# Attention row tiles: the reciprocal of a tile's sums, its spreading and its transposes, one unit later

## What is computed

```python
q, k, v = proj(Wq, bq), proj(Wk, bk), proj(Wv, bv)
scores = jnp.einsum('bhqd,bhkd->bhqk', q, k) * SCALE
scores = scores * (adj_matrix + bond_matrix)[:, None, :, :]
attn = jax.nn.softmax(scores, axis=-1)
ctx = jnp.einsum('bhqk,bhkd->bhqd', attn, v)
out = jnp.einsum('bse,fe->bsf', ctx, Wo) + bo
```

## Time and profile before

| | us |
|---|---|
| median of 3 runs | 2968.77 |
| lowest and highest | 2966.88 and 2968.87 |
| the profiled execution | 2966.04 |
| its span, first to last instruction | 2962.9 |
| TensorE busy | 2841.6 (96%) |
| VectorE busy | 1856.5 (63%) |
| ScalarE busy | 1486.9 (50%) |
| GpSimd busy | 721.2 (24%) |

### The profile page before, as it was taken

One profiled execution on the slowest core, in us unless ns is written; L12 is line 12 of the kernel. 1 busy time (PEld: TensorE's weight loads), 2 busy tenths in 40 slices (PEclk: granted clock), 3 DMA queues, 4 the chain that ended last, 5 costly groups with the idle time before them and its releaser, 6 DMA issues.

```text
span 2962.9 us, 62026 instructions
## 1 busy us (share of the span) xinstructions
PE 2841.6 (96%) x21888; PEld 2255.5 (76%) x21888; DVE 1856.5 (63%) x4010; ACT 1486.9 (50%) x2761; POOL 721.2 (24%) x1305
## 2 busy tenths in 40 slices
PE   8999999999999999999999999999999999999999
PEld 6777787787877878778687786877868778687786
DVE  3787427874288742887428864388643886438862
ACT  2883318833288232873228732387323873238622
POOL 0342003420034201342013420134101441014410
PEclk9999999999999999999999999999999999999999
DMA  5552215522165131651316513155122551226500
GB/s 176 186 165 93 90 61 191 162 91 107 50 201 168 69 129 39 201 178 49 136 45 197 181 50 122 63 189 180 63 101 77 189 181 65 82 81 197 169 8 15
DMA packets 198987, 355.12 MB, mean 120 GB/s; under 512 B 22033, under 2 KB 126865, under 8 KB 198673
## 3 DMA queue, kind: packets, MB, share of 16 engines
q1 hardware_dynamic: 197136, 346.81, 35.1%
q0 software_dynamic: 1536, 4.20, 0.4%
HBM read 212.25 MB, written 84.15 MB: 100 GB/s over the span
## 4 chain that ended last, share of the span: by engine, by line
PE 70%; DVE 15%; issue 8%; ACT 3%; SPq 2%; DMA 1%; DVEq 1%; POOL 0%; ACTq 0%; POOLq 0%
PE ps L1265 37%; PE ps L1488 7%; PE ps L1431 7%; PE ps L1551 7%; PE ps L1453 6%; PE ps L1626 4%; DVE junk L974 3%; SPq L508 2%; DVE Z L930 2%; DVE stats L748 1%; DVE h L990 1%; DVE dn L983 1%; DVE h L1008 1%; PE ps L1305 1%; DVE shiftB L1005 1%
## 5 line engine op out<-in xcount | busy, mean ns | idle before, releaser
L1431 PE MATMUL ps<-kS,qS 128*128 128x512 f32 x1024 | 381.4, 455 | 77.8 <-DVE nm L930 74.4
L930 DVE CUSTOM_DVE_ANT_0 Z<-ps,adjN 128x1024 f32<-128x1024 f32 x328 | 394.6, 1208 | 39.4 <-PE ps L1431 35.5
L1188 ACT ACTIVATE Z<-Z,nm 128x1024 f32<-128x1024 f32 x328 | 378.3, 1157 | 18.4 <-POOL nm L685 18.4
L697 POOL TENSOR_SCALAR H<-adjN 128x128 fp32r<-128x128 f32 (+1 forms) x456 | 317.8, 697 | 0.0
L1431 PEld LDWEIGHTS ps<-kS,qS 128*128 128x128 f32 x1024 | 160.6, 189 | 164.8 <-DVE nm L930 124.3
L1178 ACT ACTIVATE PTa<-ps 128x512 f32<-128x512 f32 x448 | 246.6, 599 | 75.2 <-PE ps L1453 62.6
L1453 PE MATMUL ps<-ident,Z 128*128 128x128 f32 x1920 | 253.2, 274 | 6.0 <-ACT Z L1188 4.3
L1453 PEld LDWEIGHTS ps<-ident,Z 128*128 128x128 f32 x1920 | 219.3, 140 | 49.7 <-issue 19.6
L685 POOL TENSOR_TENSOR nm<-nm,minus 128x1 f32<-128x1 f32 x512 | 98.2, 192 | 571.7 <-DVE nm L930 570.7
L930 DVE CUSTOM_DVE_ANT_0 Zx<-ps,adjN 128x1024 f32<-128x1024 f32 x184 | 221.3, 1205 | 8.8 <-PE ps L1431 6.9
L1265 PE MATMUL ps<-mh,adjT 128*128 128x256 f32 x1024 | 223.6, 379 | 0.8 <-issue 0.8
(11 more groups left out here) (192 smaller groups left out, 6215.4 us busy)
## 6 DMA issues: line engine op xcount, KB each, us to landing
blocks_kept<-blocks_in SPq DMA_DIRECT2D x144, 512.0 KB, 3.0
blocks_even<-blocks_kept SPq DMA_DIRECT2D x288, 128.0 KB, 3.4
adjT<-adjT_in SPq DMA_DIRECT2D x8, 4096.0 KB, 13.4
adjN<-adj_in SPq DMA_DIRECT2D x8, 4096.0 KB, 15.6
PTb<-blocks_kept SPq DMA_DIRECT2D x192, 128.0 KB, 3.5
adjT<-adjT_in SPq DMA_DIRECT2D x8, 2048.0 KB, 9.1
qS<-qhi SPq DMA_DIRECT2D x112, 128.0 KB, 2.1
qS<-qlo SPq DMA_DIRECT2D x112, 128.0 KB, 2.1
```

Source lines behind the costliest of these rows:

```text
L697: done = pool.tensor_scalar(H[:, t, of], adjN[:, t, of], 0.0, 0.0, ALU.is_equal, ALU.is_equal)
L930: dve.tensor_tensor_reduce(Z_of(u), ps[:, 2 * (u % 2):2 * (u % 2) + 2].rearrange("p a n -> p (a n)"), adjN[:, u // HEADS], SCORE_SCALE, LO ...
L1188: act.activation(Z_of(u), Z_of(u), ACT.Exp, bias=nm[:, u:u + 1], accum_out=sm[:, HEADS * (u // HEADS) + place(u):HEADS * (u // HEADS) + pl ...
L1431: mm = pe.matmul(ps[:, 2 * (u % 2) + s], qS[:, hd, rows(t)], kS[:, hd, half(s)], start=True, stop=True)
```

## The change

Two of the lags go from 4 to 5. INVERT sets the step of the reciprocal on VectorE and of the spreading on GpSimd, SPREAD that of the two transposes on TensorE. So for tile t all three are due at step 8t + 9 and no longer at step 8t + 8; each keeps its place within a step. The copy out of PSUM and all that uses the inverses stay where they are.

```diff
-        INVERT, SPREAD, COPY, WEIGH, NORMALISE, PROJECT, ADD = 4, 4, 7, 7, 9, 10, 11
+        INVERT, SPREAD, COPY, WEIGH, NORMALISE, PROJECT, ADD = 5, 5, 7, 7, 9, 10, 11
```

## The result

The changed kernel took 2980.67 us (median of 7 runs, 2976.46 to 2987.57) against 2968.77 (7 runs, 2966.88 to 2970.8): a ratio of 1.0041, 95% interval 1.003 to 1.0052. It is 11.9 us slower; the forecast was 2971.1 us, 2.3 slower, with a range up to 2979. The profiled execution took 2983.07 us with a span of 2981.0, 18.1 more than before. It is one of the slower of the seven, and it lists a mean granted TensorE clock of 0.994, where the one before lists 1.000; the seven runs lie between 0.994 and 0.997. None of that was in the forecast.

The account below looks back on a forecast made before the run. The prediction took a ring of waits between engines, 15.80 us per tile, as the bound. A batch gains 0.81 and loses 1.1, +0.3 us; eight batches add 2.3 to 2968.77, giving 2971.1 us, range 2963 to 2979.

Parts of the forecast that it names:

- The stall before the reciprocal is nearly covered: At middle tile boundaries, VectorE's 1.15 us idle mostly hides behind TensorE's transposes; only 0.09 us is to spare.
- parts 1 and 2: Boundaries after tiles 2 to 5 gain 0.09 us each, 0.36 a batch; tile 1 to 2 gains 0.35 us.
- The rival that the 75.4 us come back: VectorE's 1.15 us return whole at five boundaries a batch: -40 us, 2929 us; chance 0.10 together with an in-between case.
- part 3: Boundary of tile 6 to 7, where TensorE sets the pace: scores start 0.10 us earlier, bounds 0 and 0.22.
- part 4: Batch's tail: spreading stands behind GpSimd's 3.64 us incidence, delaying TensorE; loses 1.1 us a batch, bounds 0.7 and 2.07.
- The weighted values (1.88) run from 960.7 to 962.6: Tail, TensorE: last tile's weighted values take 1.88 us behind the late spreading transposes, so first edges start at 962.6.
- the sign of being wrong: Prediction is wrong if the tail costs above 1.6 or below 0.7 us, or the beat falls over 0.2 us.
- The slower rival: Tail, GpSimd's steps 64 and 65: late spreading delays TensorE by 2.07 us, not 1.1; +10.1 us, 2978.9 us; chance 0.29.
- The race between the spreading and the first h: Tail: GpSimd's spreading and VectorE's h start within 0.15 us; 0.1 us added, 0.4 more if h always went first.

## Why the prediction was wrong

- **The stall before the reciprocal is nearly covered (parts 1 and 2): right.** The wait moved to the eviction (0.81 us, plus 0.26 at the added output; the forecast had about 0.6), the beat fell from 15.80 to 15.73 where 15.71 was forecast, and tile 1 to 2 gained 0.34 us in seven batches where 0.35 was forecast. Only the last batch gave less: 0.19 us there, and nothing at the boundaries behind. The rival that the 75.4 us come back is out.
- **Tile 6 to 7 (part 3): too high.** 0.10 us was forecast; between the negations of units 52 and 60, which lie on either side of this boundary, 0.01 us or less was gained. All gains sum to 4.6 us in the profiled execution, 0.57 a batch against 0.81.
- **The tail by order (part 4): right.** 1.18 us a batch against 1.1; the spreading's transposes came 6.82 us behind unit 63's negation, where 960.4 - 953.64 = 6.8 was meant, and the first edges followed the weighted values, as forecast. With the gains it gives the +5 us that the four added products leave.
- **The step that failed: "The weighted values (1.88) run from 960.7 to 962.6".** They took 3.54 us, at a granted clock of 0.57. The sum took the 2 us of new wait as time in which nothing else changes, and priced the work behind it from rows at the full clock. The granted clock is in the view of stretches, and 1.00 stood in the stretch that was read the earlier trace rows; no row showed what it does behind a wait of 2 us, and its effect was put at nothing without a reason. The edge products behind, which the forecast called gapless for 11.22 us, took 11.23. The term left out is 1.46 us of tail in seven of eight batches of the profiled execution, 10.2 us. For the median run it is an estimate: without it the measured terms give 2968.8 + 4.8 = 2973.6, inside the range, and 2980.67 is 7 us above that; no trace of that run shows it. The tail of the profiled execution grew by 2.6 us in seven batches, above the 1.6 that the prediction named as the sign of being wrong.
- **The slower rival named the right place and the wrong mechanism.** It gave 2978.9 us for hh and hl coming late. They did not hold up the first edges: in the changed kernel these follow the weighted values at once, and what made those late beyond the forecast was the clock. Its number was near by chance.
- **The race between the spreading and the first h** was worth little: two h took 0.91 us, and the spreading its usual 0.86. The reading behind it, that an h is held for as long as the incidence runs, is refuted by the kernel with the incidence behind the spreading. There the first h ran at 0.41 us in the midst of it.

## What to carry to other kernels

When a step is moved one place later, read what it now stands behind on each engine's queue, at the last pass of the loop above all, where other work is placed: five boundaries gained 0.6 us a batch together, two gained nothing, and the last lost up to 2.6. A wait that becomes longer on TensorE is not priced by its length alone: the work right behind it may run at half clock, and a few products that nobody reads, put into the wait, show at once whether it does. A stall of 75 us on a well-filled engine can be worth 5, if the engine catches up with another one a few instructions later.

## What the runs showed of the hardware

- The granted clock fell behind a wait of 1.97 to 2.01 us with little work around it, in seven of eight batches of the changed kernel and of the one with the last tile alone. In the one batch of each that was spared, the wait was as long (2.01 and 1.99 us). With 1.89 us of work put in its place the clock never fell in a tail. In the kernel before, TensorE's longest wait from 20 us on was 1.24 us, for VectorE's maxima, and the clock stayed at 1.00 throughout. In the kernel with the late incidence it stayed at 1.00 behind seven waits of 1.81 us and fell behind one of 1.99. What spared those two batches is not shown.
- VectorE and GpSimd hold each other up, but not as I read it. The Trainium skill ("SBUF — State Buffer", section "SBUF: two separate sides") has a shared pair of ports locked for a whole instruction. These runs agree only in part. In the kernel before, the first h was issued 0.82 us before the incidence's end and ran until 0.15 us behind it. With the incidence behind the spreading, three h and two hl (which have two SBUF inputs) ran at 0.41 to 0.43 us each in the midst of the same 3.65 us instruction. Held were the one issued just behind its start (0.81 for 0.14) and the one issued 0.44 us before its end (0.59, again until 0.15 us behind it). Eight pieces in its place hold nothing of VectorE's back, and themselves take up to 0.75 us for 0.64. What decides who waits stays open.
- A 128x256 product of plain float32 operands took 0.43 us: eight of them stand in the trace as 16 rows in 3.62 us, four as 8 rows in 1.89 us. The distance of two neighbouring rows in a chain, 0.22 us, is half of it. The scores, whose operands are declared float32r, stand with one row for each product (1024 for 512 units of two). So the 64 instructions of the weighted values, in rows for a group of four heads, are 32 products.
